# Gated attention on one Trainium2 core: the scaling of O is moved behind the last lows of P

## The chip, the cores and the metric

The kernel runs on one core of a Trainium2 chip. Time is device microseconds of one execution, from the first instruction to the end of the last. Times of a kernel are given as the median of several runs; a profile is one more execution, recorded instruction by instruction.

## The reference, cut to what matters

Two layers, each of gated cross attention and a gated feed-forward part, all in float32. The change touches only the attention. For each of 8 batches, with 112 latent rows `x` and 375 context rows:

```python
kv = concatenate([context, latents], axis=1)             # 487 rows
q = latents @ Wq; k = kv @ Wk; v = kv @ Wv               # layer 0: q and k also RMS-normed
scores = einsum("bhgqd,bhkd->bhgqk", qg, k) * scale
probs = softmax(scores)
out = einsum("bhgqk,bhkd->bhgqd", probs, v)              # O
x = x + tanh(gate) * (out @ Wo)
```

Layer 0 has 32 query heads on 8 key/value heads of dimension 128; layer 1 has 16 on 4 of dimension 96. So four query heads share a key/value head in both.

## The kernel before, in words

Float32 accuracy on TensorE is made of three passes: each operand is cut into a high part (rounded) and a low part (the rest), and `product` issues high*high, low*high, high*low. Cutting costs one copy (high) and one subtraction (low) for every operand, spread over ScalarE, VectorE and GpSimd.

`attend` runs the attention of one layer in **units**: a unit `u` is one key/value head with one batch, with its four query heads; layer 0 has U = 64 units and layer 1 has U = 32. Eight units (the eight batches, `k = u % 8`) are a **group** `g`. Each engine runs its own written-out order for iteration `u`, and semaphores tie them. All of it is software-pipelined: iteration `u` works on the scores of unit `u+1`, on P of unit `u`, and on the last two products of unit `u-1`.

TensorE in iteration `u`: scores of heads 0 and 1 of unit `u+1`; transposes of P, key tiles 0 and 1 of unit `u` (`turn`); the transpose of the inverted row sums (`turn_sums`, which waits for `invert` on VectorE); an "early" output-projection piece if `g >= 1` and `k >= 1`; scores of heads 2 and 3 (head 3 waits for the first `exp`); `multiply(u-1, 2)` and `(u-1, 3)`, after which O of unit `u-1` is whole in PSUM; in layer 1 the transposes of a slab of Wo (`turn_slab`, six units of eight); `turn(u, 2)` and `(u, 3)`; `multiply(u, 0)` and `(u, 1)`; a "late" projection piece if `g >= 1` and `k <= 6`. So the units of the first group of a layer have no projection piece at all.

VectorE in iteration `u`: `neg_max(u+1, 0)` (L1768), `invert(u)` (L1775), `neg_max(u+1, 1)`, `low(u, 0)`, `low(u, 1)` (L1787), `cut_k(u+2)` (L1782), the add of the early piece, `neg_max(u+1, 2)`, `(u+1, 3)`, then `take_o(u-1)`, in layer 1 `cut_slab` (L1814), `low(u, 2)`, `low(u, 3)`, the add of the late piece (L1809). `take_o` multiplies O in PSUM by the inverted row sums `rb`: one instruction of 128x448 in layer 0 (L1795), and in layer 1 three of 32x112 (L1800) and one of 96x336 (L1801), because there heads of 96 rows are laid out into 128.

ScalarE in iteration `u`: `exp(u+1, 0)` (L1692), `high(u, 0)`, `high(u, 1)` (L1714), `exp(u+1, 1)`, `copy_sums(u)` (L1700), `cut_q(u+2)` (L1707), `exp(u+1, 2)`, `exp(u+1, 3)`, `cut_slab` (L1732 in layer 0, L1729 in layer 1), `high(u, 2)`, `high(u, 3)`, and last `cut_o(u-1)` (L1721), the high part of the scaled O.

GpSimd in iteration `u`: `cut_k(u+2)` (L1530), `cut_q(u+2)` (L1525), in layer 0 `cut_slab` (L1550), `cut_v(u+1)` (L1537, L1539), and last `cut_o(u-1)` (L1545), the low part.

SyncE issues the loads in order: `load_qk(u+3)`, `load_v(u+2)`, `spread_sums(u)` (the inverted sums to DRAM, L1485), a slab of Wo, and `fetch_sums(u)` (L1491), which reads them back broadcast over the partitions into `rb`, two units in turn. In layer 0 `rb` is also where `take_o` writes, so `fetch_sums(u)` waits for `o_lo >= u-1`, the low part of O of unit `u-2`; in layer 1 it waits for `o_taken >= u-1`. In units 1 to 7 of layer 0 a load of `x` follows.

Of the kernel before, what the change touches and what calls it, by code (L numbers as in the profile page):

```python
# [74 lines left out]
def flamingo(nc, x, ctx4096, g_xattn, g_ffn, wq0, wk0, wv0, wo0, qw0, kw0, wffn0,  # L75
# [38 lines left out]
    with stack:  # L114
# [1220 lines left out]
        def attend(n, L, wo, x_sb, place, banks, ready, source=None, tail_count=4):  # L1335
# [5 lines left out]
            D, U, NB = L.d, L.units, BATCH  # L1341
# [21 lines left out]
            def slabs_by(u):  # L1363

                return sum(1 for w in range(u) if w % NB in SLAB_AT)
# [6 lines left out]
            def late_of(u):  # L1372

                g, k = u // NB, u % NB
                return PIECES * (g - 1) + 2 * k if g and k < NB - 1 else None
# [141 lines left out]
            def gpsimd(pool):  # L1517
                ready.room(pool)
                pool.memset(kr[:, :, KVLEN:KVPAD], 0.0).then_inc(padded, 1)
                pool.memset(vr[:, :, CT, :], 0.0).then_inc(padded, 1)  # L1520

                def cut_q(u):
                    p = u % 2
                    pool.wait_ge(q_hi, u + 1)
                    pool.tensor_tensor(qs[:, p, 1, :], qr[:, p, :], f32(qs[:, p, 0, :]), ALU.subtract).then_inc(q_cut, 1)  # L1525

                def cut_k(u):
                    p = u % 2
                    pool.wait_ge(k_hi, u + 1)
                    pool.tensor_tensor(ks[:, p, 1, :], kr[:, p, :], f32(ks[:, p, 0, :]), ALU.subtract).then_inc(k_cut, 1)  # L1530

                def cut_v(u):
                    p = u % 2
                    if u >= 2:
                        pool.wait_ge(multiplied, KVT * (u - 1))
                    pool.wait_ge(v_loaded[p], 32 * (u // 2) + 32)
                    pool.tensor_copy(vs[0:CR, p, 0, :, :], vr[0:CR, p, :, :]).then_inc(v_hi, 1)  # L1537
                    pool.wait_ge(v_hi, u + 1)
                    pool.tensor_tensor(vs[0:CR, p, 1, :, :], vr[0:CR, p, :, :], f32(vs[0:CR, p, 0, :, :]), ALU.subtract).then_inc(v_cut, 1)  # L1539

                def cut_o(u):
                    g, b, p = u // NB, u % NB, u % 2
                    cols = slice(b * QLEN, (b + 1) * QLEN)
                    pool.wait_ge(o_hi, u + 1)
                    pool.tensor_tensor(ol[g % 2][:, :, cols], on[:, p, :, :], f32(oh[g % 2][:, :, cols]), ALU.subtract).then_inc(o_lo, 1)  # L1545

                def cut_slab(w):
                    i, j = w // NK, w % NK
                    pool.wait_ge(w_hi_s, w + 1)
                    pool.tensor_tensor(w_lo[i % 3][:, j, :], raw[:, w % RAW, :], f32(w_hi[i % 3][:, j, :]), ALU.subtract).then_inc(w_lo_s, 1)  # L1550

                cut_q(0)
                cut_v(0)
                cut_k(1)
                cut_q(1)
                yield
                for u in range(U):
                    if u + 2 < U:
                        cut_k(u + 2)
                        cut_q(u + 2)  # L1560
                    if not flip and u % NB in SLAB_AT:
                        cut_slab(slabs_by(u))
                    if u + 1 < U:
                        cut_v(u + 1)
                    if u:
                        cut_o(u - 1)
                cut_o(U - 1)

            def tensor(pe):
# [116 lines left out]
            def scalar(act):  # L1686
                def exp(u, h):
                    m, p = G * u + h, u % 2
                    act.wait_ge(maxed, m + 1)
                    if h == 0 and u >= 2:  # L1690
                        act.wait_ge(turned, KVT * (u - 1))
                    act.activation(pr[:, p, h, 0:KVLEN], score_bank(m)[0:QLEN, 0:KVLEN], ACT.Exp, bias=nmax[:, p, h:h + 1],  # L1692
                                   accum_out=rsum[:, p, h:h + 1]).then_inc(exped, 1)

                def copy_sums(u):
                    p = u % 2
                    act.wait_ge(r_turned, u + 1)
                    if u >= 2:
                        act.wait_ge(r_stored[p], 16 * (u // 2))
                    act.activation(rt[:, p, :], o[p][0:G, 0:QLEN], ACT.Copy).then_inc(r_copied, 1)  # L1700

                def cut_q(u):
                    p = u % 2
                    if u >= 2:
                        act.wait_ge(scored, G * (u - 1))
                    act.wait_ge(qk_loaded[p], 48 * (u // 2) + 48)
                    act.activation(qs[:, p, 0, :], qr[:, p, :], ACT.Copy).then_inc(q_hi, 1)  # L1707

                def high(u, x):
                    m, r = KVT * u + x, ROWS[x]  # L1710
                    act.wait_ge(turned, m + 1)
                    if u:
                        act.wait_ge(multiplied, m - KVT + 1)
                    act.activation(pt_hi[0:r, x, :], tb[x % 2][0:r, :], ACT.Copy).then_inc(hi_done, 1)  # L1714

                def cut_o(u):
                    g, b, p = u // NB, u % NB, u % 2
                    act.wait_ge(o_taken, u + 1)
                    if g >= 2 and b == 0:
                        act.wait_ge(projected, PIECES * (g - 1))  # L1720
                    act.activation(oh[g % 2][:, :, b * QLEN:(b + 1) * QLEN], on[:, p, :, :], ACT.Copy).then_inc(o_hi, 1)  # L1721

                def cut_slab(w):
                    i, j = w // NK, w % NK
                    if i >= 3 and j == 0:
                        act.wait_ge(projected, TT * (i - 2))
                    if flip:
                        act.wait_ge(w_turned, w + 1)
                        act.activation(w_hi[i % 3][:, j, :], y[:], ACT.Copy).then_inc(w_hi_s, 1)  # L1729
                    else:  # L1730
                        act.wait_ge(raw_loaded[w % RAW], 16 * (w // RAW) + 16)
                        act.activation(w_hi[i % 3][:, j, :], raw[:, w % RAW, :], ACT.Copy).then_inc(w_hi_s, 1)  # L1732

                cut_q(0)
                yield
                for h in range(G):
                    exp(0, h)
                    yield
                cut_q(1)
                yield  # L1740
                ready.space(act)
                for u in range(U):
                    more = u + 1 < U
                    if more:
                        exp(u + 1, 0)
                    high(u, 0)
                    high(u, 1)
                    if more:
                        exp(u + 1, 1)
                    copy_sums(u)  # L1750
                    if u + 2 < U:
                        cut_q(u + 2)
                    if more:
                        exp(u + 1, 2)
                        exp(u + 1, 3)
                    if u % NB in SLAB_AT:
                        cut_slab(slabs_by(u))
                    high(u, 2)
                    high(u, 3)
                    if u:  # L1760
                        cut_o(u - 1)
                cut_o(U - 1)

            def vector(dve):
# [19 lines left out]
                def low(u, x):  # L1784
                    m, r = KVT * u + x, ROWS[x]
                    dve.wait_ge(hi_done, m + 1)
                    dve.tensor_tensor(pt_lo[0:r, x, :], tb[x % 2][0:r, :], f32(pt_hi[0:r, x, :]), ALU.subtract).then_inc(lo_done, 1)  # L1787
# [37 lines left out]
                for u in range(U):  # L1825
                    more = u + 1 < U
                    if more:
                        neg_max(u + 1, 0)
                    invert(u)
                    if more:  # L1830
                        neg_max(u + 1, 1)
                    low(u, 0)
                    low(u, 1)
                    if u + 2 < U:
                        cut_k(u + 2)
                    if early_of(u) is not None:
                        add(early_of(u), y)
                    if more:
                        neg_max(u + 1, 2)
                        neg_max(u + 1, 3)  # L1840
                    if u:
                        take_o(u - 1)
                    if flip and u % NB in SLAB_AT:
                        cut_slab(slabs_by(u))
                    low(u, 2)
                    low(u, 3)
                    if late_of(u) is not None:
                        add(late_of(u), y)
                take_o(U - 1)
# [801 lines left out]
```

## Time and profile before

| | |
|---|---|
| median of 3 runs | 2707.05 us (2704.16 to 2710.39) |
| the profiled execution: time, span | 2703.99 us, 2702.2 us |
| mean granted clock of TensorE | 0.993 |
| TensorE matmul busy | 2629.9 us, 97% of the span |
| TensorE weight loads busy | 2242.5 us, 83% |
| VectorE busy | 1530.5 us, 57% |
| ScalarE busy | 1290.0 us, 48% |
| GpSimd busy | 1040.8 us, 39% |
| 64 units of layer 0, first to last L1795 | 1194.4 to 1900.5 us |
| 32 units of layer 1, first L1800 to last L1801 | 2318.0 to 2625.9 us |

A matmul's end in such a profile is modelled, and matmuls overlap, so that a busy share near 100% does not show that TensorE ran at its peak. The columns of a timeline row are start, duration, engine, line, operation, tiles, count, and in brackets the idle time of the engine before the instruction with what ended it. Two instructions of one engine may overlap by about 0.1 us in their records.

### The profile page before, as it was taken

To read this page: it belongs to the slowest core of one execution; us is meant where nothing else is said; L and a number is where in the kernel's file an instruction comes from. 1 tells how busy PE (TensorE), PEld (TensorE's weight loads), DVE (VectorE), ACT (ScalarE), POOL (GpSimd) and SP (SyncE) were. 2 spreads that over 40 slices of the span, in tenths; PEclk is the share of its full clock that TensorE was granted. 3 is DMA by queue.
4 is the path that set the end of the run, shared out by engine and by line. 5 is a ranking of instruction groups with operands and counts; after the bars stand their busy time and mean duration, and the time that the engine had idled before them with its cause. 6 is when DMAs were issued, how large, how long until landed. Compare 5 with 4: busy or idle time off the path is not lost. (4 is left out here: it accounts for less than half of the span.)

```text
span 2702.2 us, 38854 instructions
## 1 busy us (share of the span) xinstructions
PE 2629.9 (97%) x13508; PEld 2242.5 (83%) x13508; DVE 1530.5 (57%) x2710; ACT 1290.0 (48%) x2846; POOL 1040.8 (39%) x882
## 2 busy tenths in 40 slices
PE   7999999999899999999999999999889999999998
PEld 6788778888898888877888888888788989788887
DVE  7767785444655333356656656665465311777776
ACT  6655664333444333366545555554252312755544
POOL 2555424576262111146555555555020000544430
PEclk9999999999999999999999999999999999999999
DMA  4566565465543323346333333332420232433311
GB/s 169 186 210 202 165 229 202 159 207 176 189 149 128 98 89 102 99 121 179 107 100 105 109 105 103 108 107 77 143 60 1 73 98 79 121 93 81 90 42 55
DMA packets 337897, 332.21 MB, mean 123 GB/s; under 512 B 127104, under 2 KB 275320, under 8 KB 337704
## 3 DMA queue, kind: packets, MB, share of 16 engines
q1 hardware_dynamic: 336616, 327.63, 38.9%
q8 instruction: 110, 1.80, 0.3%
q10 hardware_dynamic: 1088, 2.10, 0.2%
q14 instruction: 83, 0.68, 0.1%
HBM read 233.16 MB, written 96.49 MB: 122 GB/s over the span
## 5 line engine op out<-in xcount | busy, mean ns | idle before, releaser
L45 PE MATMUL pb<-p_ws,p_xs 128*128 128x512 f32 (+1 forms) x1124 | 436.4, 388 | 22.7 <-DVE p_xs L461 8.6
L47 PE MATMUL pb<-p_ws,p_xs 128*128 128x512 f32 (+1 forms) x1124 | 427.1, 380 | 0.0
L46 PE MATMUL pb<-p_ws,p_xs 128*128 128x512 f32 (+1 forms) x1124 | 426.2, 379 | 0.0
L823 POOL TENSOR_TENSOR p_xr<-p_xf 128x512 f32<-128x512 f32 x175 | 245.1, 1418 | 271.4 <-ACT p_xf L1019 162.5
L1692 ACT ACTIVATE at_p<-pb,at_nmax 112x487 f32<-112x487 f32 x256 | 171.5, 672 | 314.0 <-DVE at_nmax L1768 313.9
L1224 DVE TENSOR_TENSOR p_c<-pb,p_c 128x512 f32<-128x512 f32 (+1 forms) x280 | 175.6, 658 | 188.8 <-PE pb L47 188.0
L45 PEld LDWEIGHTS pb<-p_ws,p_xs 128*128 128x128 f32 x1124 | 212.5, 189 | 60.1 <-issue 15.3
L1530 POOL TENSOR_TENSOR at_k<-at_kr,at_k 128x488 fp32r<-128x488 f32 (+1 forms) x94 | 116.3, 1238 | 372.9 <-DVE at_k L1782 372.9
L47 PEld LDWEIGHTS pb<-p_ws,p_xs 128*128 128x128 f32 x1124 | 212.1, 189 | 36.4
L46 PEld LDWEIGHTS pb<-p_ws,p_xs 128*128 128x128 f32 x1124 | 212.7, 189 | 32.5
L1787 DVE TENSOR_TENSOR at_ptlo<-pb,at_pthi 125x448 fp32r<-125x448 f32 (+1 forms) x256 | 147.9, 620 | 80.5 <-ACT at_pthi L1714 80.3
L1809 DVE SCALAR_TENSOR_TENSOR x_sb<-pb,gates,x_sb 128x512 f32<-128x512 f32 x112 | 84.1, 751 | 185.1 <-PE pb L47 185.1
L45 PE MATMUL pb<-p_w,p_xq 128*128 128x512 f32 x448 | 179.7, 401 | 1.5 <-DVE p_c L1224 1.5
L45 PE MATMUL pb<-at_whi,at_oh 128*128 128x512 f32 x448 | 179.4, 400 | 0.0
L461 DVE TENSOR_TENSOR p_xs<-p_xr,p_xs 128x512 fp32r<-128x512 f32 x175 | 164.7, 966 | 26.0 <-ACT p_xs L1037 26.0
L47 PE MATMUL pb<-p_w,p_xq 128*128 128x512 f32 x448 | 175.3, 391 | 0.0
L47 PE MATMUL pb<-at_whi,at_ol 128*128 128x512 f32 x448 | 175.1, 391 | 0.0
L46 PE MATMUL pb<-at_wlo,at_oh 128*128 128x512 f32 x448 | 174.7, 390 | 0.0
L46 PE MATMUL pb<-p_w,p_xq 128*128 128x512 f32 x448 | 174.5, 390 | 0.0
L1768 DVE TENSOR_REDUCE at_nmax<-pb 112x1 f32<-112x487 f32 x256 | 167.8, 661 | 1.9 <-PE pb L47 1.9
L1525 POOL TENSOR_TENSOR at_q<-at_qr,at_q 128x448 fp32r<-128x448 f32 (+1 forms) x96 | 110.7, 1154 | 134.9 <-ACT at_q L1707 134.9
L1056 ACT ACTIVATE p_c<-pb 128x512 f32<-128x512 f32 (+1 forms) x158 | 83.2, 573 | 158.3 <-PE pb L47 158.3
(264 smaller groups left out, 6461.2 us busy)
## 6 DMA issues: line engine op xcount, KB each, us to landing
p_xf<-xT_d SPq DMA_DIRECT2D x23, 1024.0 KB, 5.6
p_raw<-in_L_xattn_Wq_dram SPq DMA_DIRECT2D x32, 512.0 KB, 4.2
at_raw<-in_L_xattn_Wo_dram SPq DMA_DIRECT2D x64, 256.0 KB, 2.7
xT_d<-p_xf SPq DMA_DIRECT2D x15, 1024.0 KB, 5.1
qT_d<-p_qstage SPq DMA_DIRECT2D x56, 256.0 KB, 2.7
at_qr<-qT_d SPq DMA_DIRECT2D x64, 224.0 KB, 3.1
at_rb<-rT_d SPq DMA_DIRECT2D x64, 224.0 KB, 3.4
at_kr<-kT_d SPq DMA_DIRECT2D x64, 187.5 KB, 2.9
```

The costliest lines, as they stand in the source:

```text
L45: pe.matmul(out, stat_hi, mov_hi, start=start, stop=False)
L46: pe.matmul(out, stat_hi, mov_lo, start=False, stop=False)
L47: return pe.matmul(out, stat_lo, mov_hi, start=False, stop=stop)
L461: eng.tensor_tensor(xs[:, n % 10, 1, :, :], src, f32(xs[:, n % 10, 0, :, :]), ALU.subtract).then_inc(signal, 1)
L823: pool.tensor_tensor(xr[:, n % 10, 1, :, :], src[:, a[0], HK * a[1]:HK * a[1] + HK, :], src[:, b[0], HK * b[1]:HK * b[1] + HK, :], op).the ...
L1224: dve.tensor_tensor(cb[:, p % 2, c, 0:wide(w)], yb[j][:, 0:wide(w)], cb[:, p % 2, c, 0:wide(w)], ALU.add).then_inc(c_add, 1)
L1525: pool.tensor_tensor(qs[:, p, 1, :], qr[:, p, :], f32(qs[:, p, 0, :]), ALU.subtract).then_inc(q_cut, 1)
L1530: pool.tensor_tensor(ks[:, p, 1, :], kr[:, p, :], f32(ks[:, p, 0, :]), ALU.subtract).then_inc(k_cut, 1)
L1692: act.activation(pr[:, p, h, 0:KVLEN], score_bank(m)[0:QLEN, 0:KVLEN], ACT.Exp, bias=nmax[:, p, h:h + 1], accum_out=rsum[:, p, h:h + 1]).t ...
L1768: dve.tensor_reduce(nmax[:, p, h:h + 1], score_bank(m)[0:QLEN, 0:KVLEN], AX.X, ALU.max, negate=True).then_inc(maxed, 1)
L1787: dve.tensor_tensor(pt_lo[0:r, x, :], tb[x % 2][0:r, :], f32(pt_hi[0:r, x, :]), ALU.subtract).then_inc(lo_done, 1)
L1809: dve.scalar_tensor_tensor(out=cols, in0=bank[:], scalar=gate, in1=cols, op0=ALU.mult, op1=ALU.add).then_inc(added, 1)
```

## The change

`take_o(u-1)` on VectorE goes from behind `neg_max(u+1, 3)` to behind `low(u, 3)`. The high part of that O on ScalarE goes from the end of iteration `u` to the middle of the next one, behind `high(u, 1)`, where it is `cut_o(u-2)`; its low part on GpSimd is `cut_o(u-2)` too, and stands ahead of `cut_v(u+1)`. Two such cuts stand behind the loop instead of one. No instruction is added or taken away, and TensorE's and SyncE's orders are the same.

```diff
 def gpsimd(pool):
@@ for u in range(U)
                         cut_slab(slabs_by(u))
+                    if u >= 2:
+                        cut_o(u - 2)
                     if u + 1 < U:
                         cut_v(u + 1)
-                    if u:
-                        cut_o(u - 1)
+                cut_o(U - 2)
                 cut_o(U - 1)
 def scalar(act):
@@ for u in range(U)
                     high(u, 0)
                     high(u, 1)
+                    if u >= 2:
+                        cut_o(u - 2)
                     if more:
                         exp(u + 1, 1)
                     copy_sums(u)
...
                     high(u, 2)
                     high(u, 3)
-                    if u:
-                        cut_o(u - 1)
+                cut_o(U - 2)
                 cut_o(U - 1)
 def vector(dve):
@@ for u in range(U)
                         neg_max(u + 1, 3)
-                    if u:
-                        take_o(u - 1)
                     if flip and u % NB in SLAB_AT:
                         cut_slab(slabs_by(u))
                     low(u, 2)
                     low(u, 3)
+                    if u:
+                        take_o(u - 1)
                     if late_of(u) is not None:
                         add(late_of(u), y)
                 take_o(U - 1)
```

## Rows read from the trace of the kernel before

**Rows 1.** Busy time in three stretches: both first groups, and layer 0's later ones.

```profile
1188.71:1248.30 59.59, 53.29 (x290) 42.99 (x289) 38.79 (x78) 43.44 (x112) 46.72 (x44) 0.97 0.66 194
1270.00:1890.00 620.00, 620.00 (x3290) 534.84 (x3289) 373.49 (x675) 324.92 (x847) 346.19 (x314) 1.00 0.36 104
2313.44:2365.31 51.87, 51.53 (x307) 41.44 (x306) 46.94 (x105) 41.00 (x110) 31.32 (x34) 1.00 0.47 122
```

**Rows 2.** Timeline of VectorE in one iteration of layer 1's first group.

```profile
2313.44 0.66 DVE L1768 TENSOR_REDUCE at_nmax<-mid_pb 112x1 f32<-112x487 f32 x1
2314.01 0.17 DVE L1775 RECIPROCAL at_rinv<-at_rsum 112x4 f32<-112x4 f32 x1
...
2318.01 0.84 DVE L1800 TENSOR_TENSOR at_on<-mid_pb,at_rb 32x112 f32<-32x112 f32 x3
...
2319.37 0.69 DVE L1814 TENSOR_TENSOR at_wlo<-mid_pb,at_whi 128x512 fp32r<-128x512 f32 x1
2319.97 1.15 DVE L1787 TENSOR_TENSOR at_ptlo<-mid_pb,at_pthi 125x448 fp32r<-125x448 f32 x2
2321.04 0.66 DVE L1768 TENSOR_REDUCE at_nmax<-mid_pb 112x1 f32<-112x487 f32 x1
```

**Rows 3.** Timeline of ScalarE in the same iteration.

```profile
2315.64 0.68 ACT L1692 ACTIVATE at_p<-mid_pb,at_nmax 112x487 f32<-112x487 f32 x1
...
2317.44 0.67 ACT L1692 ACTIVATE at_p<-mid_pb,at_nmax 112x487 f32<-112x487 f32 x1 [0.45 <-DVE at_nmax L1768]
...
2318.74 0.60 ACT L1729 ACTIVATE at_whi<-mid_pb 128x512 fp32r<-128x512 f32 x1
...
2320.06 0.51 ACT L1721 ACTIVATE at_oh<-at_on 128x336 fp32r<-128x336 f32 x1
```

**Rows 4.** Timeline of TensorE in the same iteration: the transpose of the sums.

```profile
2314.24 0.26 PE L1595 MATMUL mid_pb<-ident,at_rinv 112*4 112x112 f32 x1
```

**Rows 5.** Timeline of VectorE in layer 1, units 15 and 16 (k = 7, then 0).

```profile
2449.70 0.84 DVE L1800 TENSOR_TENSOR at_on<-mid_pb,at_rb 32x112 f32<-32x112 f32 x3 [0.55 <-PE mid_pb L47]
...
2450.98 1.14 DVE L1787 TENSOR_TENSOR at_ptlo<-mid_pb,at_pthi 125x448 fp32r<-125x448 f32 x2
2452.39 0.67 DVE L1768 TENSOR_REDUCE at_nmax<-mid_pb 112x1 f32<-112x487 f32 x1 [0.27 <-PE mid_pb L47]
...
2461.48 0.75 DVE L1809 SCALAR_TENSOR_TENSOR x_sb<-mid_pb,gates,x_sb 128x512 f32<-128x512 f32 x1 [1.40 <-PE mid_pb L47]
```

**Rows 6.** Timeline of ScalarE in the first of those two units.

```profile
2450.13 0.98 ACT L1714 ACTIVATE at_pthi<-mid_pb 125x448 fp32r<-125x448 f32 x2 [0.18 <-PE mid_pb L1587]
```

**Rows 7.** Timeline of VectorE in one iteration of layer 0's first group.

```profile
1203.66 0.66 DVE L1768 TENSOR_REDUCE at_nmax<-pb 112x1 f32<-112x487 f32 x1
...
1210.96 0.62 DVE L1795 TENSOR_TENSOR at_rb<-pb,at_rb 128x448 f32<-128x448 f32 x1 [2.76 <-DMA at_rb<-rT_d]
1211.50 1.15 DVE L1787 TENSOR_TENSOR at_ptlo<-pb,at_pthi 125x448 fp32r<-125x448 f32 x2
1212.56 0.66 DVE L1768 TENSOR_REDUCE at_nmax<-pb 112x1 f32<-112x487 f32 x1
```

**Rows 8.** What VectorE waited for, 1183 to 1248 us: total, times, longest.

```profile
DVE at_rb L1795 <- DMA at_rb<-rT_d: 15.3, 7, 3.3
```

**Rows 9.** Timeline of SyncE's queue in the same stretch: sums stored and fetched.

```profile
1206.40 0.34 SPq L1491 DMA_DIRECT2D at_rb<-rT_d  x1
...
1211.09 0.32 SPq L1485 DMA_DIRECT2D rT_d<-at_rt  x1
...
1215.12 0.34 SPq L1491 DMA_DIRECT2D at_rb<-rT_d  x1
```

**Rows 10.** Timeline of GpSimd in the iteration of rows 7.

```profile
1209.67 1.30 POOL L1550 TENSOR_TENSOR at_wlo<-at_raw,at_whi 128x512 fp32r<-128x512 f32 x1 [0.20 <-ACT at_whi L1732]
...
1212.83 1.15 POOL L1545 TENSOR_TENSOR at_ol<-at_rb,at_oh 128x448 fp32r<-128x448 f32 x1
```

**Rows 11.** Timeline of VectorE in a later unit of layer 0 with a late piece.

```profile
1331.07 0.75 DVE L1809 SCALAR_TENSOR_TENSOR x_sb<-pb,gates,x_sb 128x512 f32<-128x512 f32 x1 [2.38 <-PE pb L47]
```

## The prediction

> **What bounds the kernel now.** I read the busy times by stretch first, then the waits, then the timelines of single iterations, engine by engine. TensorE is busy 97% of the span, so a change to VectorE's order can matter only where TensorE is paced by others. In layer 0 from the second group on, matmuls cover 620.00 of 620 us and weight loads 86.3% of it (534.84 / 620) [rows 1]: TensorE is full, and the other engines only have to keep up. The two first groups, which have no projection pieces, look different: weight loads fill 79.9% of layer 1's (41.44 / 51.87) and 72.1% of layer 0's (42.99 / 59.59) [rows 1]. Those two stretches, 7 iterations each (1 to 7), are where the change is decided.
>
> The reader is to see one loop in layer 1's first group. From one `neg_max(u+1, 0)` to the next it is 2321.04 - 2313.44 = 7.60 us, and VectorE goes from the second low straight into it: lows start at 2319.97, the next `neg_max` at 2321.04, 1.07 us later, with no idle time [rows 2]. Everything follows from that instruction: the first exp, the highs, the first lows, `cut_k`, the other maxima, exps 2 and 3, the slab's copy on ScalarE at 2318.74, its subtraction on VectorE at 2319.37 (0.63 after the copy's start), the lows, and round again [rows 2, 3]. TensorE hangs on it too: its transpose of the sums starts at 2314.24, 0.06 us after `invert` ends at 2314.18 [rows 2, 4]. The sum of matmul time would hide this: it is 51.53 of 51.87 us there [rows 1]. By that alone TensorE would be the bound, the move would cost nothing in layer 1, and the sum below would end at -1.1; by the share of weight loads, which is 6 points under the full stretch, something else sets the pace, and the sum ends at +9.1. I go by the loop that the timeline shows. The Trainium skill (Perfetto Trace Analysis, Identifying the Most-Contended Engine) says the same of the measures, that matmul busy time is a bad one because pipelined matmuls overlap and the weight loads' share is to be used; the trace agrees so far as 79.9% against 86.3%.
>
> Layer 0's first group is paced by something else. VectorE waits there 7 times, 15.3 us in all, for the fetched sums, standing in `take_o` ahead of the last two lows [rows 8]. SyncE's queue makes that wait: sums of a unit are stored at 1211.09, fetched at 1215.12 when they have landed, and the fetch before was at 1206.40, a cycle of 8.72 us made of issues and one round trip, with nothing computed in it that is late [rows 9]. The mean iteration is 59.59 / 7 = 8.51 us [rows 1].
>
> **The change part by part.** No instruction is added. What moves:
>
> *take_o away from the lows, layer 1.* Its cost in VectorE's queue: at least 2450.98 - 2449.70 = 1.28 us, and 2319.37 - 2318.01 = 1.36 us as an upper value, where the slab's copy ends the interval [rows 2, 5]. I take 1.28, since the first interval ends with VectorE's next work ready. Does its leaving let slab and lows go earlier? The slab's subtraction starts 0.63 us after the copy on ScalarE, which follows exp 3, and the exps follow the maxima; `take_o` ended at that same moment. So the gain is taken as nothing; its bounds are 0 and the 0.08 between the two prices. If the slab's copy were not there, the gain would be up to the whole 1.28.
>
> *take_o behind the lows, layer 1's first group.* There it stands directly ahead of `neg_max(u+2, 0)`, which had no idle time [rows 2], so the loop takes 1.28 us more: 7.60 becomes 8.88. Behind it in VectorE's queue are `neg_max`, `invert` and the second `neg_max`; ScalarE's first exp waits for the first, TensorE's transpose of sums for the second, and TensorE's last score for the exp. Seven iterations: **+8.96 us**. Bounds: 0, if TensorE really is full, and 7 x 1.36 = 9.5.
>
> *The same in layer 1's later groups.* With a late piece, VectorE idles 1.40 us before the add of it [rows 5]; 1.28 fits. That row is the tightest kind, behind a unit without one. If that cover were gone, each such unit would pay up to 1.28. Where `k = 7` there is no late piece: `neg_max` came 0.27 us of idle after the lows, at 2452.39. Without `take_o` ahead, the lows can start 0.57 to 0.6 after the high at 2450.13 (the high takes that long until VectorE may subtract), say 2450.72 instead of 2450.98; plus 1.07 for the lows and 1.28 for `take_o` gives 2453.07, which is 0.68 late [rows 2, 5, 6]. The next unit (`k = 0`) has its slab's low ahead of the late piece, so it starts from `neg_max` as in the loop above, and TensorE inherits the delay. Two boundaries (units 15 and 23): **+1.4 us**; bounds 0 and 2 x 1.28 = 2.6.
>
> *Layer 0's first group.* `take_o` costs 1211.50 - 1210.96 = 0.54 us of queue [rows 7]. Behind the lows it would lengthen a loop like layer 1's to 7.60 + 0.54 = 8.14 us, still under the 8.51 that the fetches allow. What changes is what stands behind the landing: before, landing, `take_o`, two lows, `neg_max` (1212.56 - 1210.96 = 1.60 us) [rows 7]; now landing, `take_o`, `neg_max` (0.54). The two lows are done while the fetch is under way. As the fetches run by themselves, this is not 1.06 us per unit but once: VectorE runs 1.06 us closer behind the same fetches. **-1.06 us**; bounds: 0, and if the fetches too went faster, 7 x (8.51 - 8.14) = 2.6 plus that, -3.7.
>
> *cut_o on ScalarE.* Its record is 0.51 us in layer 1 [rows 3]. It now stands ahead of `exp(u+1, 1)`; behind it are that exp, `copy_sums`, `cut_q` and exp 2, and exp 2 had 0.45 us of idle, ended by VectorE's maximum [rows 3]. Records of ScalarE overlap by about 0.1 (an exp's 0.68 and the rest are back to back), so that the queue time is some 0.4 to 0.5: hidden, cost 0; upper bound 0.06 per iteration and, for layer 0, as much again, about 1 us over both first groups.
>
> *cut_o on GpSimd, and SyncE.* Now ahead of `cut_v(u+1)`, which is 1.15 us later [rows 10] and needed only in the next iteration. In layer 0 `fetch_sums(u)` waits for the low part of O of unit `u-2`, now made in iteration `u` behind the slab's low. It ends at the earliest at 1209.67 + 1.30 + 1.15 = 1212.12, 8.46 us after the iteration's start at 1203.66 [rows 7, 10]; that fetch went out at 1215.12 [rows 9], 3.0 us later. The fetch before it, at 1206.40, has less: its iteration started some 7.6 us before 1203.66, will start 0.54 later than that, and 8.46 on is 1205.1, still 1.3 us early. Behind `fetch_sums` stand `load_qk(u+4)`, `load_v(u+3)`, the next store and the next slab. In later groups they are issued later than now, by no more than the part of an iteration between the sums and the slab's low, for units that are two iterations ahead: cost 0.
>
> *Layer 0's later groups.* VectorE idles 2.38 us before the add of the late piece [rows 11]: 0.54 is hidden. Without a late piece the delay is 0.54 less some idle, below the time that TensorE needs for its next transposes: 0.
>
> **Sum.** 8.96 + 1.4 - 1.06 = +9.3, rounded down to +9.2 for a little of the 0.08. Against the profiled execution: 2703.99 + 9.2 = 2713.2. The median of the runs shown is 3.06 higher, so 2707.05 + 9.2 = **2716.2 us**.
>
> **The rivals.**
>
> *TensorE is nearly full in layer 1 (no change).* The matmul record speaks for it; the loop without idle time speaks against it. If half the +8.96 is absorbed by room elsewhere and the boundaries cost nothing: 4.5 - 1.06 = +3.4, 2710.5 us.
>
> *Faster: the first groups are TensorE's.* Place: layer 0's first group. There VectorE no longer holds the last lows back behind a landing, and TensorE waits for just those lows. If that wait was the pace, and not SyncE's cycle, the group falls to the length at which its weight loads fill 86.3%: 42.99 / 0.863 = 49.8 us, 9.8 less [rows 1]; with `take_o` free in layer 1 the time is 2697.3. It decides from the point where the fetches come closer together than 8.1 us. Against it: VectorE's own loop allows 8.14, not 7.1.
>
> *Slower still: ScalarE's cut is not hidden.* If queue time is the whole record, exp 2 is late by 0.51 - 0.45 or more, and if the exps are late in the loop by a full cut, 7 x 0.51 in each layer's first group, 7 us more: 2723. For it: the idle time is as long as the cut, to 0.1 us. Against: records overlap.
>
> **How the numbers follow.** Forecast 0.72, half absorbed 0.12, faster 0.07, ScalarE's cut in the loop 0.09. The range goes from between forecast and no change to just short of the last: 2709 to 2722. A measurement of this kernel tells about 0.2% (5.4 us) from no change. Slower by more: forecast, last rival, less a tail: 0.79; within: 0.14; faster: 0.07.
>
> **What would show it.** In the profile after: iterations of layer 1's first group of 8.9 us where they are 7.6, with `take_o` back to back between the lows and `neg_max`; the stretch of 51.87 us about 60.8. Layer 0's first group about 58.5 us instead of 59.59, the wait for the sums still there, but behind the lows. Later groups unchanged but for 0.7 us at two boundaries. Exp 2 still released by the maximum. I am wrong if layer 1's iterations stay near 7.6, if layer 0's fetches are spaced otherwise than 8.7 us, or if `fetch_sums` is seen waiting for GpSimd.

## The result and the profile after

| | before | after |
|---|---|---|
| median of 19 runs each | 2703.88 us (2701.02 to 2710.39) | 2712.61 us (2709.93 to 2720.47) |
| ratio | | 1.0033, 95% interval 1.0026 to 1.0040 |
| the profiled execution: time, span | 2703.99, 2702.2 us | 2718.28, 2716.5 us |

The change costs 0.33%, 8.9 us (7.0 to 10.8). Of the runs made for the experiments below, two disturbed ones (3708.78 and 9305.18 us) are left out of the ratios. The profiled execution of the kernel after is one of its longest, 5.7 us over the median, so its span is not to be compared with the one before as a whole; its stretches are. Busy times in layer 0's first group, in its later groups and in layer 1's first group, the first and last from one `neg_max(u+1, 0)` to another as in [rows 1]; the columns are stretch, length, then busy time and count of TensorE's matmuls and weight loads, VectorE, ScalarE, GpSimd, then granted clock, DMA share, GB/s:

```profile
1194.01:1254.30 60.29, 52.09 (x295) 42.34 (x294) 38.98 (x78) 42.25 (x111) 45.63 (x43) 1.00 0.64 188
1278.00:1898.00 620.00, 620.00 (x3289) 535.48 (x3289) 367.96 (x675) 324.13 (x847) 346.52 (x314) 1.00 0.37 103
2319.31:2380.82 61.51, 53.50 (x315) 42.15 (x313) 47.04 (x104) 40.52 (x109) 31.73 (x34) 1.00 0.42 108
```

The reader is to see one row changed: layer 1's first group is 61.51 us long where it was 51.87 [rows 1], with the same work in it. Layer 0's later groups are full as before. The chain of VectorE in one iteration there:

```profile
2328.29 0.65 DVE L1770 TENSOR_REDUCE at_nmax<-mid_pb 112x1 f32<-112x487 f32 x1
...
2331.59 1.23 DVE L1770 TENSOR_REDUCE at_nmax<-mid_pb 112x1 f32<-112x487 f32 x2
2334.20 0.69 DVE L1816 TENSOR_TENSOR at_wlo<-mid_pb,at_whi 128x512 fp32r<-128x512 f32 x1 [1.39 <-ACT at_whi L1730]
2334.81 1.15 DVE L1789 TENSOR_TENSOR at_ptlo<-mid_pb,at_pthi 125x448 fp32r<-125x448 f32 x2
2335.99 0.84 DVE L1802 TENSOR_TENSOR at_on<-mid_pb,at_rb 32x112 f32<-32x112 f32 x3
2336.84 0.50 DVE L1803 TENSOR_TENSOR at_on<-mid_pb,at_rb 96x336 f32<-96x336 f32 x1
2337.26 0.65 DVE L1770 TENSOR_REDUCE at_nmax<-mid_pb 112x1 f32<-112x487 f32 x1
```

From one first maximum to the next it is 8.97 us, where it was 7.60 [rows 2]; the two iterations of the seven that have no slab take 8.33 and 8.32, where they took 6.95 and 6.94. Each of the seven is thus 1.37 to 1.39 us longer. The place that the scaling left is now 1.39 us of idle time that ScalarE's copy of the slab ends, so nothing moved up into it; and the scaling stands between the lows and the next maximum. TensorE shows the same, in the list of its waits for 2300 to 2380 us and in its timeline:

```profile
PE mid_pb L1596 <- DVE at_rinv L1777: 7.6, 6, 1.4
```

```profile
2338.05 0.26 PE L1596 MATMUL mid_pb<-ident,at_rinv 112*4 112x112 f32 x1 [1.36 <-DVE at_rinv L1777]
```

It waits for `invert`, which is queued behind the maximum. In the kernel before no such wait was listed, though the transpose followed `invert` by 0.06 us there too [rows 2, 4]: the loop was already the pace, without a gap to show it.

ScalarE in the same iteration, where the high part of O now stands ahead of the second exp:

```profile
2329.63 0.97 ACT L1715 ACTIVATE at_pthi<-mid_pb 125x448 fp32r<-125x448 f32 x2
2330.48 0.49 ACT L1722 ACTIVATE at_oh<-at_on 128x336 fp32r<-128x336 f32 x1
2330.85 0.68 ACT L1693 ACTIVATE at_p<-mid_pb,at_nmax 112x487 f32<-112x487 f32 x1
...
2331.64 0.56 ACT L1708 ACTIVATE at_q<-at_qr 96x448 fp32r<-96x448 f32 x1
2332.28 0.67 ACT L1693 ACTIVATE at_p<-mid_pb,at_nmax 112x487 f32<-112x487 f32 x1
```

The cut takes 0.37 us of the queue (2330.85 - 2330.48). Exp 2 starts 0.69 us behind the maximum that it needs (2331.59 to 2332.28), as before (from the first of the two maxima below to the 2317.44 of [rows 3]).

```profile
2316.75 1.23 DVE L1768 TENSOR_REDUCE at_nmax<-mid_pb 112x1 f32<-112x487 f32 x2
```

The idle time is used up and no more.

In layer 0's first group VectorE now waits for the sums behind the lows:

```profile
1224.38 1.15 DVE L1789 TENSOR_TENSOR at_ptlo<-pb,at_pthi 125x448 fp32r<-125x448 f32 x2 [1.86 <-ACT at_pthi L1715]
1226.09 0.62 DVE L1797 TENSOR_TENSOR at_rb<-pb,at_rb 128x448 f32<-128x448 f32 x1 [0.55 <-DMA at_rb<-rT_d]
1226.63 0.66 DVE L1770 TENSOR_REDUCE at_nmax<-pb 112x1 f32<-112x487 f32 x1
```

```profile
DVE at_rb L1797 <- DMA at_rb<-rT_d: 4.0, 4, 1.5
```

The wait for a landing is 4.0 us in all where it was 15.3 [rows 8], and the maximum follows the landing by 0.54 us and not by 1.60 [rows 7]. And yet the group is 60.29 us long, not shorter than 59.59. The gain is there at its end. These are the last fetch that the group needs and the maximum that ends it, first before and then after:

```profile
1241.99 0.34 SPq L1491 DMA_DIRECT2D at_rb<-rT_d  x1
...
1248.30 0.65 DVE L1768 TENSOR_REDUCE at_nmax<-pb 112x1 f32<-112x487 f32 x1
```

```profile
1249.07 0.34 SPq L1491 DMA_DIRECT2D at_rb<-rT_d  x1
...
1254.31 0.65 DVE L1770 TENSOR_REDUCE at_nmax<-pb 112x1 f32<-112x487 f32 x1
```

That is 6.31 us before and 5.24 after, 1.07 less. The other profiles agree: 6.10 to 6.40 in four more kernels with the scaling of layer 0's first group in its old place, 5.04 to 5.23 in three more with it behind the lows. But the fetches themselves took longer in this execution. One cycle of SyncE's queue:

```profile
1221.48 0.34 SPq L1491 DMA_DIRECT2D at_rb<-rT_d  x1
...
1224.48 1.80 SPq L1463 DMA_DIRECT2D at_vr<-vl_d  x1
1226.32 0.33 SPq L1485 DMA_DIRECT2D rT_d<-at_rt  x1
...
1230.86 0.34 SPq L1491 DMA_DIRECT2D at_rb<-rT_d  x1
```

From fetch to fetch it is 9.38 us here, the longest of seven cycles (7.74 to 9.38, mean 8.77); in the kernel before the cycles are 7.45 to 9.08, mean 8.65, with 8.72 in [rows 9]. This is scatter and not the change: with VectorE's and both cuts' order in layer 0 as before, the mean is 8.82 and 8.83 us in two other profiles, and with the scaling moved it is 8.76 to 8.81 in three. The first iterations are paced by VectorE instead, until the fetches fall behind: two of 7.48 and 7.47 us before, three of 7.99 after, so the moved scaling is paid there, and the fetches swallow it.

In this cycle GpSimd is not what the fetch waits for: the low part of O that must be ready was done long before.

```profile
1223.99 1.29 POOL L1550 TENSOR_TENSOR at_wlo<-at_raw,at_whi 128x512 fp32r<-128x512 f32 x1 [0.20 <-ACT at_whi L1733]
1225.24 1.14 POOL L1545 TENSOR_TENSOR at_ol<-at_rb,at_oh 128x448 fp32r<-128x448 f32 x1
```

It ends at 1226.38, and the store before that fetch, whose landing the fetch waits for too, went out at 1226.32. SyncE's waits at its fetches from 1194 to 1256 us:

```profile
SPq L1491 <- DMA rT_d<-at_rt: 23.1, 7, 3.7
SPq L1490 <- POOL at_ol L1545: 0.7, 1, 0.7
```

The second one is at the fetch of 1212.83: SyncE is free at 1209.68, the low part of O ends at 1210.41, and the landing is waited for 2.4 us more. So a fetch is seen waiting for GpSimd, but the landing comes last, and the wait costs nothing. In layer 0's later groups, from 1300 to 1890 us, such waits are long and many:

```profile
SPq L1490 <- POOL at_ol L1545: 285.9, 50, 6.0
```

They cost nothing where they are: that stretch is full on TensorE, and its iterations take 12.37 to 12.39 us where they took 12.37 and 12.38.

### The profile page after: what moved, and what is told of

Same layout as the page of the kernel before. It is cut to its first block and busy times, and to the rows that moved or that the text cites. A ratio compares the mean times of both kernels' runs of the same rounds, so it can differ in the third digit from the quotient of the medians.

```text
span 2716.5 us, 38854 instructions
## 1 busy us (share of the span) xinstructions
PE 2629.5 (97%) x13508; PEld 2242.2 (83%) x13508; DVE 1534.6 (56%) x2710; ACT 1285.6 (47%) x2846; POOL 1036.1 (38%) x882
```

## The experiments

The theory: the loss is the queue time of `take_o` between the last low and the next first maximum, in the units without a late piece in layer 1; in layer 0 SyncE's fetches hide it; the cuts cost nothing. Rivals: layer 0's fetches, delayed by GpSimd; ScalarE's cut; a gain from the old place that the loss hides. Every ratio below is to the kernel before, run beside it.

**Layer 1 alone, layer 0 alone.** The three moves made under a condition (`flip` is true in layer 1):

```diff
-                    if u:
+                    if u and not (flip):
                         take_o(u - 1)
...
                     low(u, 3)
+                    if u and flip:
+                        take_o(u - 1)
```

and the same for both `cut_o`; for layer 0 with `not flip`.

> The whole change (the scaling of O and its two cuts) in layer 1 alone; layer 0 as before. Theory (the loss is the scaling standing in VectorE's queue between the last low and the next maximum of layer 1's first group): the whole loss of the change or a little more, 11 us (9.6 in the 7 iterations of the first group, 1.5 at two boundaries): ratio 1.004; iterations of 8.97 us there. Rival (the loss comes from layer 0, where a fetch of sums now waits for GpSimd): ratio within 0.1% of 1.

> The whole change in layer 0 alone; layer 1 as before. Theory: the fetches of sums keep their spacing of 8.7 us, VectorE's start of an iteration comes 1.06 us closer behind a landing, so -1 us: ratio 0.9996, within 0.1% of 1. Rival (the later low part of O delays the fetches): +2 us or more, ratio 1.001, and fetches farther apart than 8.8 us.

Layer 1 alone: 1.0031 (1.0022 to 1.0041), 8.4 us (5.9 to 11.1), where 11 were expected. Layer 0 alone: 0.9995 (0.9986 to 1.0003), -1.3 us (-3.8 to +0.8). The loss is layer 1's. Its first group with the change in that layer alone, from the profile:

```profile
2311.91:2373.45 61.54, 53.54 (x316) 42.29 (x314) 47.06 (x105) 40.58 (x109) 31.75 (x34) 1.00 0.42 108
```

This repeats the 61.51 to 0.03 us. Layer 0's first group is no such constant. With VectorE's order in layer 0 as before it took 59.59, 61.04 and 61.16 us in three profiles (and 61.72 and 62.44 in two where only the cuts were moved); with the scaling moved 60.29, 60.72, 59.43 and 59.82. The granted clock does not sort the lengths: it was 0.97 in those of 59.59, 59.82, 61.04 and 61.16 us, and 1.00 in those of 59.43, 60.29 and 60.72. From `invert(1)` to `invert(63)`, which holds the end of the group too, the means of the three and of the four are 705.4 and 705.0 us, each with a scatter of 1 to 2. The sign of layer 0's part in the total is thus not shown by these; the rival's +2 us is out for the time (its interval ends at +0.8).

**The scaling alone, the cuts alone.**

> The scaling of O moved in both layers, its high and low part left at the end of the iteration. Theory (all of the price is VectorE's): the time of the changed kernel, ratio 1.0033 to the kernel before; iterations of 8.97 us in layer 1's first group. Rival (the cuts on ScalarE in the middle of the iteration delay the exps): 1 to 3 us less than the changed kernel, and the iterations under 8.9 us.

> The two cuts of O moved into the next iteration, the scaling left where it was. Theory: nothing, ratio 1.000 within 0.1%, exp 2 still released by VectorE's maximum and iterations of 7.60 us in layer 1's first group. Rival (ScalarE's cut of 0.5 us is not hidden): up to 7 us more, ratio 1.0026, with iterations of up to 8.1 us.

The scaling alone: 1.0037 (1.0025 to 1.0049), iterations of 8.97 us: the whole loss. The cuts alone: 1.0006 (0.9997 to 1.0014). That interval holds both nothing and 3.8 us; the profile is sharper, since layer 1's first group has its old length with the cuts moved:

```profile
2318.28:2370.12 51.84, 51.49 (x307) 41.44 (x306) 46.94 (x104) 40.57 (x109) 30.56 (x33) 1.00 0.47 123
```

One part of its expectation missed: exp 2 is no longer shown as released by VectorE after idle time. It starts right behind `cut_q` (in the timeline shown last here), 0.68 us after its maximum's start as ever (2329.18 to 2329.86), so the cut fills the idle time and does not lengthen the loop of 7.59 us. In layer 0's first group, 61.72 us there, SyncE's fetches meet the moved low part of O three times, 1.4 us in all. These waits are hidden too: the low parts end at 1205.63, 1213.38 and 1222.21, and the landings are waited for 2.1, 3.2 and 3.6 us more, until the fetches of 1207.76, 1216.61 and 1225.83. The kernel of the next experiment has one such wait, of 1.2 us, and 2.4 us of landing behind it. So they are not the 1.1 and 1.8 us by which the two groups with only the cuts moved (61.72 and 62.44) exceed the mean of the three old ones (60.60). Whether that is more than scatter stays open.

```profile
SPq L1490 <- POOL at_ol L1545: 1.4, 3, 0.8
```

```profile
2329.23 0.56 ACT L1711 ACTIVATE at_q<-at_qr 96x448 fp32r<-96x448 f32 x1
2329.86 0.67 ACT L1696 ACTIVATE at_p<-mid_pb,at_nmax 112x487 f32<-112x487 f32 x1
```

**Only where there is a late piece.** The changed cuts; the scaling behind the lows `if late_of(u) is not None`, else in its old place.

> The changed kernel, but with the scaling of O behind the last lows only in units that have a late projection piece, and in its old place in all others. Theory (VectorE's idle time before the add of a late piece, 1.4 us in layer 1 and 2.4 in layer 0, covers the scaling, and only the units without such a piece pay): the time of the kernel before, ratio 1.000 within 0.1%. Rival (the scaling costs in every unit of layer 1, some 0.1 us or more in each of 21): 2 us or more, ratio 1.001.

0.9997 (0.9988 to 1.0007). The rival's 2 us or more is just outside this interval, which ends at 1.9. In the profile layer 1's later iterations have their old lengths, 11.49, 11.46 and 11.00 us, and so have the boundaries, 8.95 and 8.96, and 9.73 to 9.75 behind them. The idle time before the late add covers the scaling in all 21 such units of layer 1 and the 49 of layer 0. Only the units without a late piece pay.

**The work of the scaling taken out, at either place.** `take_o` in layer 1, from the third unit on, is one instruction of 96x8, so that layer 1's output lacks the scaling:

```diff
                         dve.wait_ge(o_lo, u - 1)
+                    if u >= 2:
+                        dve.tensor_tensor(on[0:D, p, 0, 0:8], ov[:, 0, 0:8], rb[:, p, 0, 0:8], ALU.mult).then_inc(o_taken, 1)
+                        return
                     for j in range(NK):
```

> The kernel before, with the scaling of O in layer 1 from its third unit on cut down to one instruction of 96x8, so that the output of layer 1 lacks it. Theory (the old place was free, since slab and lows wait for ScalarE): iterations of 7.60 us in layer 1's first group stay within 0.1 us of that, the total is at most 1 us less. Rival (the old place cost too, and its leaving was a gain): iterations of about 6.4 us, the total 8 us less, ratio 0.997.

> The changed kernel with the same cut of the scaling in layer 1. Theory (the new place charges the scaling its whole queue time): iterations of layer 1's first group fall from 8.97 to about 7.75 us, boundaries lose their 0.76 us, the total is 1 to 2 us over the kernel before, ratio 1.0005. Rival (the loss is the waits of the moved scaling or of the moved cuts, and not its work): still 9 us over the kernel before, ratio 1.003.

At the old place: 0.9993 (0.9984 to 1.0002), and the loop stays at 7.59 us. The scaling was free there, and its leaving could give nothing. At the new place: 1.0006 (0.9998 to 1.0015), a loss that can't be told from none. Its timeline shows the loop fall with the work, to a little less than the 7.75 us expected:

```profile
2344.97 0.15 DVE L1802 TENSOR_TENSOR at_on<-mid_pb,at_rb 96x8 f32<-96x8 f32 x1
2345.05 0.65 DVE L1770 TENSOR_REDUCE at_nmax<-mid_pb 112x1 f32<-112x487 f32 x1
...
2350.96 0.69 DVE L1819 TENSOR_TENSOR at_wlo<-mid_pb,at_whi 128x512 fp32r<-128x512 f32 x1 [1.39 <-ACT at_whi L1730]
2351.57 1.15 DVE L1789 TENSOR_TENSOR at_ptlo<-mid_pb,at_pthi 125x448 fp32r<-125x448 f32 x2
2352.63 0.15 DVE L1802 TENSOR_TENSOR at_on<-mid_pb,at_rb 96x8 f32<-96x8 f32 x1
2352.70 0.65 DVE L1770 TENSOR_REDUCE at_nmax<-mid_pb 112x1 f32<-112x487 f32 x1
```

2352.70 - 2345.05 = 7.65 us. The small instruction takes 0.07 us of queue, and the loop is 0.06 us over 7.59: whatever stands at this place is paid to the last tenth of a microsecond. The two iterations that still have the whole scaling take 8.97 and 8.98 (from one `invert` to the next).

**SyncE's fetch of the sums.** In layer 0, so that three issues lie inside the round trip of the sums:

```diff
                         load_qk(u + 3)
+                    if u and not flip:
+                        fetch_sums(u - 1)
                     if u + 2 < U:
                         load_v(u + 2)
...
-                    fetch_sums(u)
+                    if flip:
+                        fetch_sums(u)
```

It was run in three kernels: the one before, the changed one, and the one with the change in layer 0 alone.

> The kernel before, with one change in SyncE's order in layer 0: the fetch of the sums of unit u-1 is issued behind the loads of q and k of unit u+3 instead of ahead of them, so that these issues lie inside the round trip. Theory (layer 0's first group is paced by SyncE's cycle of issues and one round trip, 8.7 us): the fetches come 7.5 us apart, as VectorE's and ScalarE's loop allows, the 7 iterations take 53 us instead of 59.6: 6 to 8 us less, ratio 0.9974. Rival (the first group is paced by TensorE or GpSimd): ratio 1.000.

> The changed kernel with SyncE's fetch of the sums of unit u-1 behind the loads of q and k in layer 0. Theory (in layer 0 the slow fetches hid the moved scaling, and once they are quick it is paid there too): iterations of layer 0's first group of 8.00 us where the kernel before has 7.47 with the same fetch order, the group 56.0 us instead of 52.3; the total 14 to 15 us over the kernel before with that order, so 4 to 5 us over the kernel before itself: ratio 1.0016. Rival (the scaling behind the lows is free in layer 0 at any spacing of the fetches): iterations of 7.47 us, ratio 1.0003 or less.

> The change in layer 0 alone, with the same order of the fetches. Theory: 8.00 us per iteration in layer 0's first group, the total 3 to 4 us over the kernel before with that order of fetches: ratio 0.9975 to the kernel before. Rival (free at any spacing): ratio 0.996, as the kernel before with that order.

| with the earlier fetch | ratio to the kernel before | layer 0's iterations | first group |
|---|---|---|---|
| the kernel before | 0.9962 (0.9949 to 0.9975) | 7.46 to 7.47 us | 52.26 us |
| the change in layer 0 alone | 0.9983 (0.9971 to 0.9994) | 7.98 to 8.00 | 55.94 |
| the change | 1.0013 (1.0002 to 1.0025) | 7.99 to 8.00 | 55.96 |

```profile
1185.56:1237.82 52.26, 50.96 (x289) 41.59 (x288) 38.70 (x79) 42.81 (x112) 45.03 (x42) 1.00 0.80 240
```

```profile
1187.44:1243.38 55.94, 51.82 (x294) 42.20 (x293) 38.60 (x78) 42.25 (x111) 44.33 (x41) 1.00 0.76 226
```

The fetches do pace layer 0's first group. With the new order a fetch goes out every 7.46 us, the pace of the loop:

```profile
1200.62 0.38 SPq L1491 DMA_DIRECT2D at_rb<-rT_d  x1
...
1203.62 0.32 SPq L1485 DMA_DIRECT2D rT_d<-at_rt  x1
...
1208.08 0.38 SPq L1491 DMA_DIRECT2D at_rb<-rT_d  x1
```

Store to fetch is still 4.46 us, but the next loads are issued meanwhile, and in the whole first group SyncE waits for a landing once, for 0.9 us, where it waited 7 times. And once the fetches are quick, layer 0 pays for the moved scaling as layer 1 does: 0.53 us in each of 7 iterations, 3.7 us. That is shown; by the rival "free at any spacing" the group would be 52.26 us long. The first of the three kernels is the fastest of all here: 10 us (7 to 14) less than the kernel before, where 6 to 8 were expected, with `take_o` where it was.

## Why the prediction was right

It said 2716.2 us (2709 to 2722), slower with a chance of 0.79; it came to 2712.61, a loss of 8.9 us (7.0 to 10.8) where 9.2 was worked out. Of the 3.6 us between forecast and time 3.2 are the base and not the change: the three runs shown had a median of 2707.05, 19 runs have 2703.88. That the change itself came within 0.3 us of its forecast is partly luck. In the timelines layer 1 costs 11.2 us and not the 10.4 forecast, and the 1.06 us that layer 0 was to give back can't be seen in the total.

*The pace of layer 1's first group.* Right. The loop, and not the matmul record of 51.53 of 51.87 us, told where a delay counts, and the run with a 0.07 us instruction shows that there was no room at all. The rival "half absorbed" is out.

*The price there.* This term was mis-sized: 8.96 us forecast, with 9.5 as its upper bound, and 61.51 - 51.87 = 9.64 us measured, 1.38 per iteration and not 1.28. The instructions do take 1.27 (2337.26 - 2335.99). The other 0.11 is in front: `take_o` starts 1.18 us after the lows (2334.81 to 2335.99), where the maximum came 1.07 after them [rows 2]. With the 96x8 instruction, behind the same waits, the distance is 1.06, so the waits are not it. The 0.11 belongs to the first of the 32x112 instructions: it starts only when the record before it has ended, 0.03 us after it here (2334.81 + 1.15 to 2335.99) and at the old place as well (the maxima's record ends at 2317.98, the scaling starts at 2318.01 [rows 2]), where a maximum behind the lows starts 0.08 before their record ends. Why it does stays open. At the old place this was hidden, and the forecast, which read its price from the start of the scaling, left it out.

*Nothing gained at the old place.* Right, and shown by taking the work out there: 7.59 us all the same.

*Boundaries.* 1.4 us forecast for two; in the profile the iterations before them, from one `invert` to the next, take 9.72 and 9.72 us where they took 8.96, 1.52 in all, and the next unit hands the delay on, as it was worked out (9.73 and 9.73, where it was 9.76 and 9.74).

*Layer 0, -1.06 us.* The mechanism is right: the maximum follows a landing by 0.54 instead of 1.60 us, the fetches were the pace, and the end of the group comes 1.07 us closer behind its last fetch. The size of VectorE's loop was guessed too long, 8.14 us with the scaling and 7.99 measured; nothing hung on it. The group itself came to 60.29 us and not to the 58.5 named as a sign. That the total gains 1.06 is not shown: the interval is -3.8 to +0.8 us, and the fetch cycle itself varies by more from one execution to the next.

*The cuts.* Hidden, as forecast, with less queue time (0.37 us) than the 0.4 to 0.5 assumed. The rival that had them in the loop is out by the lengths in the profile. Two of the signs named were too coarse: exp 2 is no longer listed as released by the maximum, though it starts as far behind it as before, and SyncE is seen waiting for GpSimd, which was to prove the forecast wrong and does not, since the landing comes last.

*The sum of the parts.* Layer 1 by the timelines costs 9.64 + 1.52 = 11.2 us, just above what the run of layer 1 alone allows (8.4, interval 5.9 to 11.1) and the run of the whole (8.9, to 10.8). With about -1 from layer 0, which is not shown in the total, the whole would be some 10 us, inside its interval. Why the medians lose less than the timelines stays open. The prediction itself names +9.1 in one place and +9.3, rounded to +9.2, in its sum; the difference is a slip without consequence.

*The faster rival.* It took layer 0's group to 49.8 us if the landings were TensorE's only brake. With the brake off, by the earlier fetch, the kernel before goes to 52.26: VectorE's and ScalarE's loop of 7.47 us is the next bound, as was held against it.

## What to carry to other kernels

An instruction has two prices in an in-order queue: what it costs where it stands, and what it would cost where it is put. Look for the one instruction whose start the other engines' next round hangs on (here the first maximum), and keep the queue in front of it empty; a place where the engine would wait for another anyway is free. Ask this of the stage with the least other work, since the full stages hide it, and look in the DMA queue for a round trip with nothing issued inside it before trusting that a stage is bound by compute.

## What the runs showed of the hardware

Matmul busy time of 99% hid a stage in which TensorE was not the pace: 51.53 of 51.87 us, yet 0.07 us added on VectorE lengthened each iteration by 0.06. With the longer loop the share is 53.50 of 61.51, although the instructions are the same.

The same stretch of layer 1 repeats from one execution to another within 0.1 us, while layer 0's first group, with DMA busy for 0.63 to 0.69 of the time, scatters over 59.4 to 61.2 us in seven kernels that differ only elsewhere, by the scaling's place or by all of the change. The last stage differs by 2.7: it took 85.12 us in the profile before, at a mean granted clock of 0.96, and 82.43 after, at 1.00.

```profile
2617.08:2702.20 85.12, 77.02 (x442) 65.29 (x441) 55.04 (x134) 37.97 (x66) 1.83 (x2) 0.96 0.13 46
```

```profile
2634.07:2716.50 82.43, 73.86 (x442) 62.55 (x441) 54.90 (x134) 38.04 (x67) 2.74 (x3) 1.00 0.13 48
```

The lower clock lies in one place, 0.72 from 2680 to 2690 us, and the rest is at 1.00 but for 0.92 in the last 12 us. So two profiles' spans can differ by 2.7 us in a stage whose instructions are the same; comparing stretches avoids it.
